# Where the node and edge matrices stand in the hyperedge loop's round

## The reference

```python
h = x @ W                                        # (8, 1024, 64)
agg = einsum('ben,bnf->bef', alpha, h)           # one row for each of 64 hyperedges
beta = sigmoid((h @ a_gn)[:, None, :] + (agg @ a_ge)[:, :, None])
all_he = elu(beta[..., None] * h[:, None, :, :] + (1 - beta[..., None]) * agg[:, :, None, :])
logits2 = where(H[None] > 0, se[:, None, :], NEG)     # H: (1024 nodes, 64 hyperedges), 0 or 1
coefs1 = softmax(logits2, axis=-1)
g = einsum('bne,benf->bnf', coefs1, all_he)
```

## Time and profile before

| | |
|---|---|
| Median of 3 runs | 941.85 us (938.7 to 942.59) |
| The profiled execution's own time | 936.75 us |
| Its span in the profile | 935.0 us |
| PE busy | 758.3 us (81% of the span) |
| DVE, ACT, POOL busy | 470.2, 299.0, 276.2 us |
| The hyperedge loop's eight rounds | from 149.9 to 239.9 us of the span |

### The profile page before, as it was taken

How to read it: one execution, slowest core, us unless ns; L and a number is a source line. 1 busy time by engine, 2 the same in 40 slices (tenths; PEclk the granted TensorE clock), 3 DMA queues, 4 the chain that set the end, 5 groups by cost and what they waited for, 6 DMA issues and landing times. The chain is left out here.

```text
span 935.0 us, 9924 instructions
## 1 busy us (share of the span) xinstructions
PE 758.3 (81%) x3454; PEld 531.3 (57%) x3454; DVE 470.2 (50%) x1063; ACT 299.0 (32%) x544; POOL 276.2 (30%) x254
## 2 busy tenths in 40 slices
PE   3957968888996289898989929998888888929990
PEld 3737856666664277332333318677777777828880
DVE  1584245777268430554736640324667667740155
ACT  2632113544562021554635421213223332111210
POOL 0530003454564400000121465002244444440045
PEclk9958987999997599999989968999999989969995
DMA  7200020000000000000000010000000000000012
GB/s 268 90 1 1 1 90 1 1 1 1 0 2 0 0 1 1 0 1 0 1 1 0 1 48 1 1 1 1 1 1 0 1 1 1 0 1 1 1 24 67
DMA packets 12948, 14.36 MB, mean 15 GB/s; under 512 B 9680, under 2 KB 9680, under 8 KB 12896
## 3 DMA queue, kind: packets, MB, share of 16 engines
q1 hardware_dynamic: 11408, 11.61, 3.9%
q10 hardware_dynamic: 1488, 2.06, 0.7%
HBM read 11.57 MB, written 2.10 MB: 15 GB/s over the span
## 5 line engine op out<-in xcount | busy, mean ns | idle before, releaser
L1309 DVE TENSOR_REDUCE arena<-PS 128x1 f32<-128x1024 f32 x64 | 75.5, 1220 | 76.3 <-PE PS L1152 76.3
L1234 ACT ACTIVATE arena<-PS,arena 128x1024 f32<-128x1024 f32 x64 | 70.8, 1110 | 72.3 <-DVE arena L1309 72.3
L163 POOL TENSOR_TENSOR LN_Y<-LN_V,CN 128x16 f32<-128x16 f32 (+1 forms) x20 | 51.3, 2564 | 101.8 <-DVE LN_V L155 101.8
L1152 PE MATMUL PS<-arena 64*128 64x512 f32 x256 | 77.5, 626 | 4.8 <-ACT arena L1234 2.5
L1429 POOL TENSOR_TENSOR arena<-arena,SY 128x256 f32<-128x256 f32 x64 | 47.4, 740 | 112.3 <-ACT SY L1484 107.5
L1484 ACT ACTIVATE SY<-PS,WT 128x256 f32<-128x256 f32 x64 | 26.9, 471 | 138.4 <-DVE AGBD L1558 71.8
L1252 POOL TENSOR_TENSOR arena<-arena 128x128 f32<-128x128 f32 x32 | 12.9, 403 | 188.0 <-DVE arena L1313 188.0
L1627 PE MATMUL PS<-WH,KH 128*128 128x512 f32 x128 | 52.9, 414 | 16.0 <-DVE AGBD L1558 8.2
L1170 PE MATMUL PS<-arena 128*64 128x512 f32 x256 | 63.5, 619 | 1.2 <-POOL arena L1252 1.1
L1152 PEld LDWEIGHTS PS<-arena 64*128 64x128 f32 x256 | 28.5, 187 | 51.4 <-issue 32.0
L1628 PE MATMUL PS<-WL,KH 128*128 128x512 f32 x128 | 52.1, 407 | 0.0
(11 more groups left out here) (259 smaller groups left out, 1602.2 us busy)
## 6 DMA issues: line engine op xcount, KB each, us to landing
arena<-in_adj_tr SPq DMA_DIRECT2D x8, 512.0 KB, 8.2
arena<-in_x_tr SPq DMA_DIRECT2D x4, 512.0 KB, 9.1
arena<-in_x_nat SPq DMA_DIRECT2D x1, 2048.0 KB, 8.3
out<-arena SPq DMA_DIRECT2D x8, 256.0 KB, 3.0
arena<-in_w SPq DMA_DIRECT2D x2, 512.0 KB, 4.5
WT<-in_weights ACTq DMA_DIRECT2D x1, 739.0 KB, 7.9
arena<-in_h_tr ACTq DMA_DIRECT2D x2, 256.0 KB, 10.5
CN<-in_consts ACTq DMA_DIRECT2D x1, 507.0 KB, 4.9
```

Of the source, the lines that this page charges most:

```text
L163: pool.tensor_tensor(LN_Y[:, at:at + n], LN_V[:, at:at + n], CN[:, C_NEGH:C_NEGH + n], ALU.pow).then_inc(ln_rstd, 1)
L1152: ins = pe.matmul(banks("S", 2 * i + par)[:, half, :], KT[q % 2][r, tile(m)], QT[q % 2][r, c], start=True, stop=True)
L1234: act.activation(EF[2 * (i % RING) + par], banks("S", 2 * i + par).rearrange("p a c -> p (a c)"), ACT.Exp, bias=NMX[:, i, par:par + 1], ac ...
L1309: dve.tensor_reduce(NMX[:, i, par:par + 1], banks("S", 2 * i + par), AX.XY, ALU.max, negate=True).then_inc(max_ready, 1)
```

## The change

It reorders the round on PE, DVE and ACT; POOL's order stays. Nothing is computed more or less.

- DVE: `from_first` and `to_last` of the next round come first in the round (they were between the mixes and the shifts), and wait for `nsg_ready` in place of `nt_ready` and `selg_ready`. `edges` comes between the mixes and the shifts of A_ and B_ (it was behind both shifts and `bend(A_)`). `logits` goes ahead of `bend(C_)`.
- PE: `turn_edges` goes ahead of `gather(t, C_)`; `small_sums` ahead of `scatter(A_)`; `gather(t_next, A_)` and `turn_nodes` ahead of `scatter(B_)`. `turn_nodes` transposes the copy NSG in place of NSF.
- ACT: the copy to SELF goes ahead of `grow(B_)`.

```diff
                 def turn_nodes():
                     for c in range(CHUNKS):
-                        ins = pe.transpose(PS[:, 6, tile(c)], NSF[:, c, :], ident)
+                        ins = pe.transpose(PS[:, 6, tile(c)], bits(NSG[:, c, :]), ident)
...
                         pe.wait_ge(ns_ready, j + 2)
                         edge_rows(t_next)
-                        pe.wait_ge(z_ready, CHUNKS * j + 1)
-                        gather(t, C_)
                         pe.wait_ge(nst_out, j + 1)
                         pe.wait_ge(est_ready, j + 2)
                         turn_edges()
-                        scatter(A_)
+                        pe.wait_ge(z_ready, CHUNKS * j + 1)
+                        gather(t, C_)
                         pe.wait_ge(self_ready, j + 2)
                         small_sums(t_next)
+                        scatter(A_)
                         pe.wait_ge(nsg_ready, j + 2)
                         pe.wait_ge(selg_ready, j + 2)
                         pe.wait_ge(z_ready, CHUNKS * j + 2)
                         gather(t_next, B_)
-                        scatter(B_)
                         pe.wait_ge(z_ready, CHUNKS * j + 3)
                         gather(t_next, A_)
                         turn_nodes()
+                        scatter(B_)
                         scatter(C_)
...
+                        dve.wait_ge(nsg_ready, j + 1)
+                        from_first(at).then_inc(ns_half, 1)
+                        dve.wait_ge(ns_half, j + 2)
+                        to_last(at).then_inc(ns_ready, 1)
                         dve.wait_ge(be_ready, j + 1)
                         mix(B_, 1)
                         mix(A_, 2)
-                        dve.wait_ge(selg_ready, j + 1)
-                        dve.wait_ge(nt_ready, j + 1)
-                        from_first(at).then_inc(ns_half, 1)
-                        shift(A_, 2)
-                        dve.wait_ge(ns_half, j + 2)
-                        to_last(at).then_inc(ns_ready, 1)
-                        shift(B_, 1)
-                        bend(A_)
                         dve.wait_ge(r_ready, j + 2)
                         dve.wait_ge(sT_ready, j + 1)
                         edges(k_next)
+                        shift(A_, 2)
+                        shift(B_, 1)
+                        bend(A_)
                         mix(C_, 3)
                         bend(B_)
                         shift(C_, 3)
                         dve.wait_ge(small_ready, j + 2)
                         dve.wait_ge(cc_ready, j + 1)
                         small_out()
-                        bend(C_)
                         dve.wait_ge(ts_ready, j + 2)
                         logits()
+                        bend(C_)
...
                         grow(A_)
-                        grow(B_)
                         act.wait_ge(sT_ready, j + 2)
                         act.wait_ge(small_ready, j + 1)
                         edges_out(SELF, self_ready)
+                        grow(B_)
```

## The result

| | Before | After |
|---|---|---|
| Median of 4 runs each | 940.86 us (938.7 to 942.59) | 973.98 us (967.11 to 976.81) |
| Ratio | 1 | 1.034, 95% interval 1.028 to 1.040 |
| The profiled execution's own time, span | 936.75, 935.0 us | 967.11, 965.3 us |

The change makes the kernel 3.4% slower, 33 us in the medians and 30.3 us between the spans of the two profiled executions. The forecast was 953.0 us, with a range to 959.0: right in sign, far too small.

A forecast was written before the change was run, and what follows sets the result against it. The prediction took PE to bound the loop, busy 9.45 of 10.69 us a round. Stalls 9.0, round 0 -0.8 and clock +3.0 gave +11.2 us on 941.85, so 953.0 us, range 946.0 to 959.0.

The forecast's parts named there:

- The order of events: Hyperedge loop round: DVE waits at edges with shifts behind, gather of chunk C after turn_edges, first scatter after small_sums.
- The sum for a round at full clock: Rounds 1 to 7 of the hyperedge loop: 11.97 us against 10.69, +1.28 each, 9.0 us for seven.
- the chain of the prediction: One round, step by step across PE, DVE, ACT and POOL, timed from T, the start of L703: 11.97 us.
- T + 0.27: Start of L655 (edge_rows) on PE, 0.27 us after L703 starts, with the node matrix ready long before.
- T + 0.68: Bound for L655's start if it waits for address registers: +1.69 us a round, 11.8 us for seven.
- the 0.41 us that the node matrix was to gain at L655: Later rounds on PE: L655 starts at T + 0.27 in place of T + 0.68; otherwise each round is 0.41 us longer.
- the prediction's rule on the sequencer: PE's sequencer queues instructions and the wait happens there, so L655 could be prepared while L703 waits: start T + 0.27.
- Round 0: First round of the loop: PE's 2.45 us wait for L745 goes, new waits come; net -0.8 us, 0 to -1.5.
- the clock: PE's granted clock falls in four of rounds 1 to 7 in place of one; three more at 1.0 us, +3.0.
- the bound of +7.7: Upper bound of the clock term: the clock falls in all seven rounds, 6 x 1.28 us.
- clock low in every round: Rival, chance 0.12: the clock falls in every later round, +15.9 us in all, 957.8 us.

The follow-up runs named there:

- fill5: The changed kernel with five matmuls of zeros between edge_rows and turn_edges on PE: 949.33 us, 1.010 of the kernel before.
- fill8: fill5 with three more matmuls of zeros where PE waits for ACT's copies of the sums: 945.17 us, 1.0036 of the kernel before.
- only_nodes: The kernel before with only the node matrix's comparisons moved to the top of the round and turn_nodes from NSG: 935.97 us, 0.9966.

## Why the prediction was wrong

**What held.** The order of events came as chained: DVE in front of `edges`, the shifts behind it, the gather of chunk C behind L783, the first L711 behind L672. The sum for a round at full clock was 11.97 us; measured are 12.07 to 12.20 (fill5, fill8), so +1.40 in place of +1.28 in rounds 1 to 6, and about 1.1 in the last (11.6 against 10.5), which is 9.5 us in place of 9.0 for seven rounds. The timeline of PE in fill8, in a round at clock 1.00, answers to the chain of the prediction:

```profile
177.90 0.39 PE L703 MATMUL PS<-zero 128*128 128x512 bf16 x1
...
178.47 0.88 PE L655 MATMUL PS<-arena 128*128 x6 [0.17 <-issue]
...
180.52 0.52 PE L665 MATMUL PS<-CN,arena 128*128 128x128 f32 x3
...
182.16 0.40 PE L671 MATMUL PS<-SM,SELF 128*128 128x17 f32 x2
...
183.63 1.12 PE L711 MATMUL PS<-arena 128*128 128x512 f32 x2
```

The small difference begins at L655. Forecast at T + 0.27, with T + 0.68 as the bound, it came at T + 0.57 here and at T + 0.60 in round 1 of the changed kernel (162.10 against 161.50). The later steps were a little shorter than chained and took most of this back: `turn_edges` start at T + 2.62 instead of T + 2.35, the small sums at T + 4.26 instead of T + 4.25, the scatter at T + 5.73 instead of T + 5.63. Of the 0.41 us that the node matrix was to gain at L655, 0.1 came. In round 7 of the changed kernel, where the address is a constant, L655 starts 0.25 us behind T (256.71 against 256.46), so most of the delay goes with the address from a register, and by the trace the prediction's rule on the sequencer did not hold for it.

**Round 0** was forecast at -0.8 and measured at -2.3 us (11.74 against 14.07), outside its bounds of 0 to -1.5. The wait of 2.45 us went as said, and the stretch at the low clock that I had carried over from the kernel before didn't come in that execution.

**The step that failed is the clock.** It said that the clock falls in four of seven rounds in place of one, three more at 1.0 us each, +3.0 us. It falls in all seven, and a round in which it falls is 2.9 to 4.5 us longer (15.0 to 16.6 against 12.1), not 1.0. Both the price and the bound of +7.7 rested on the single low stretch of before, 3.4 us long and 1.28 us dear, whereas here a stretch lasts 6.9 to 10.2 us. Seven rounds took 94.96 us (rounds 1 to 6) and 15.9 (round 7); at full clock, by fill8, they would be 72.5 and 11.6. So the clock costs 26.8 us, less the 1.3 that it cost before: **+25.5 in place of +3.0**. With -2.3 and +9.5 this makes 32.7 us, and the loop is in fact 32.6 us longer (122.6 against 90.0), against the 30.3 between the two spans (the rest of the span gave 2 back). The 33 of the medians compare other executions: the profiled ones lie 6.9 and 4.1 us under their medians. The rival "clock low in every round" named the right mechanism, with a chance of 0.12, and took over the same wrong price.

That the clock is the cause and not a companion is shown by fill5 and fill8: the same order of the work, more instructions, 25 and 29 us less. Why a low stretch lasts so much longer than in the kernel before was only read, not tested: at the low clock the matmuls of the gather and the small sums follow each other after 0.43 us in place of 0.23, and PE's records are busy all the while, 4.00 of 4.00 us, at 0.50. Windows of 4 us after, in round 1:

```profile
167.00:171.00 4.00, 4.00 (x13) 2.97 (x14) 3.39 (x8) 2.45 (x7) 2.00 (x3) 0.50 0.00 0
171.00:175.00 4.00, 4.00 (x13) 2.85 (x13) 3.19 (x4) 0.00 (x0) 2.96 (x3) 0.70 0.00 0
```

So a PE that is busy by its records does not bring the clock back at once. In what the kernel before shows at 188 to 192 us it came back after 3.4 us.

## What to carry to other kernels

When PE is the bound and its rounds are only 10 us long, price a new stall twice: once for itself, and once for what it does to the granted clock, and don't take the second price from a kernel in which the clock fell in one round only; here it was more than twice the first. In a chain PE, DVE, PE, look for the one independent piece of work that covers the trip (here a gather) before moving it. Where PE must wait anyway, matmuls that add zero are a cheap test of whether the clock is to blame. Together with the early node matrix they also gave a small gain here (0.9927); how much of it is theirs is not settled.

## What was not expected of the hardware

**The clock falls with short idle times.** No gap in front of a matmul in the changed kernel's later rounds was longer than 1.20 us in the records, and the clock fell in each of the seven. Gaps of 0.76, about 0.3 and 0.20 us left it up in six rounds of seven before. Nor is it the longest gap by itself: round 0 of the changed kernel has it too, and stayed at 1.00.

```profile
152.05 0.52 PE L665 MATMUL PS<-CN,arena 128*128 128x128 f32 x3 [1.19 <-DVE arena L749]
```

What differs there is what stands ahead: wide gathers without a pause from 145.78 to the start of the round, where a later round has L733 with its narrow matmuls and a gap of 0.98 us (0.76 where L703 has its record). Which of the two matters was not tested. The Trainium skill (TensorE: Matmul & The Clock Gate, A second HAM failure mode: psum-queue depth-cycling) describes such a fall by frequent brief pauses; the trace agrees in each of rounds 1 to 7.

**Comparisons slow down beside POOL.** With the node matrix at the top of the round, DVE's two comparisons run while POOL works, and get longer. The timeline of DVE in round 4 after (L745 took 0.61 us before), and of POOL beside it:

```profile
218.94 1.40 DVE L745 SCALAR_TENSOR_TENSOR arena<-CN,arena 128x384 f32<-128x384 f32 x1 [0.15 <-DVE arena L742]
```

```profile
218.53 1.40 POOL L894 TENSOR_TENSOR HPL<-arena,HPH 128x512 fp32r<-128x512 f32 x1
219.88 1.36 POOL L913 TENSOR_TENSOR arena<-arena,ZS 128x512 f32<-128x512 f32 x1
```

POOL's two took 1.28 and 1.04 us before. The Trainium skill (SBUF — State Buffer, SBUF: two separate sides) says that DVE and GpSimd share a pair of ports that one of them holds for a whole instruction; DVE's 0.8 us more fit with that only roughly: a wait for the end of POOL's L894 (219.93) would make L745 0.99 + 0.61 = 1.60 us long, not 1.40. For POOL as the cause speaks that inside the changed kernel the two L745 ahead of the loop, with POOL idle, take 0.62 us (one is shown), and the seven beside POOL 1.16 to 1.40:

```profile
147.62 0.62 DVE L745 SCALAR_TENSOR_TENSOR arena<-CN,arena 128x384 f32<-128x384 f32 x1 [0.18 <-DVE arena L742]
```

It costs nothing here, since DVE then waits 4 us for PE, and in only_nodes, which has the same comparisons beside POOL, a later round is 10.69 us as before.
